# Order of three stretches of a fused attention and mixture-of-experts kernel on one Trainium2 core

## What is computed

```python
x = x + tanh(g_xattn) * attention(layernorm(x), ctx)   # x: 8 x 112 x 256, ctx: 8 x 375 x 192
x = x + tanh(g_ffn) * experts(layernorm(x))            # top-1 of 8 experts, W: 8 x 256 x 256, bias
# attention: q, k, v projections with biases, softmax(q k / 4) v for 16 heads, then Wo, bo
# experts: softmax gate, argmax, place in the expert by cumulative count, dropped beyond 112
```

## Time and profile before

| what | us |
|---|---|
| median of 3 runs | 185.61 (184.95 to 186.53) |
| the profiled execution | 185.55 |
| its span, from the first to the last instruction | 183.8 |
| PE busy | 169.8 |
| DVE busy | 128.7 |
| POOL busy | 86.4 |
| ACT busy | 80.7 |

### The profile page before, as it was taken

How to read it: one execution, slowest core, us unless ns; L and a number is a source line. 1 busy time by engine, 2 the same in 40 slices (tenths; PEclk the granted TensorE clock), 3 DMA queues, 4 the chain that set the end, 5 groups by cost and what they waited for, 6 DMA issues and landing times.

```text
span 183.8 us, 4666 instructions
## 1 busy us (share of the span) xinstructions
PE 169.8 (92%) x1799; PEld 119.6 (65%) x1799; DVE 128.7 (70%) x325; ACT 80.7 (44%) x174; POOL 86.4 (47%) x112
## 2 busy tenths in 40 slices
PE   7999979997899999999999999799689989999992
PEld 2557446674587768868766886666467876468740
DVE  5878787838278859858875988895876547755642
ACT  2114131377546817645671764356357760013100
POOL 7297948346991198563027007631040057304650
PEclk9999999999999999999999999999999999999998
DMA  5995838687375357616737532886050005387220
GB/s 153 303 259 123 187 86 208 164 197 186 92 167 136 128 129 168 211 52 156 208 100 168 162 115 69 194 255 220 0 154 4 0 23 180 117 239 199 65 61 25
DMA packets 26029, 26.04 MB, mean 142 GB/s; under 512 B 9677, under 2 KB 24409, under 8 KB 26008
## 3 DMA queue, kind: packets, MB, share of 16 engines
q1 hardware_dynamic: 24322, 23.04, 48.0%
q0 software_dynamic: 864, 2.07, 3.7%
q10 hardware_dynamic: 822, 0.64, 1.3%
HBM read 8.89 MB, written 5.06 MB: 76 GB/s over the span
## 4 chain that ended last, share of the span: by engine, by line
PE 65%; DVE 13%; SPq 5%; DMA 5%; issue 4%; ACT 4%; POOL 3%; DVEq 0%; ACTq 0%; POOLq 0%
PE pj L500 9%; PE pv L576 8%; PE sT L561 7%; PE pj L517 6%; PE sc L531 6%; PE sT L832 4%; PE sc L832 3%; PE pj L813 3%; DVE nmax L1097 3%; DMA ctx_sb<-in_ctxT 3%; PE pj L509 3%; PE misc L590 3%; SPq L364 2%; DMA x_sb<-in_x 2%; SPq L358 2%
## 5 line engine op out<-in xcount | busy, mean ns | idle before, releaser
L1097 DVE TENSOR_REDUCE nmax<-sc 112x1 f32<-112x375 f32 x112 | 58.4, 539 | 23.6 <-PE sc L531 19.6
L945 ACT ACTIVATE prob<-sT 128x448 f32<-128x448 f32 (+1 forms) x96 | 50.0, 545 | 38.1 <-PE sT L561 37.5
L561 PE MATMUL sT<-q,k 128*128 128x112 bf16 x384 | 31.7, 213 | 2.6 <-ACT prob L945 2.0
L1412 POOL TENSOR_SCALAR ve<-mv 112x1 f32<-112x1 f32 (+2 forms) x12 | 2.9, 238 | 66.2 <-DVE mv L1167 58.9
L531 PE MATMUL sc<-k,q 126*128 126x375 bf16 x104 | 31.7, 325 | 1.5 <-DVE nmax L1097 1.3
L561 PEld LDWEIGHTS sT<-q,k 128*128 128x128 bf16 x384 | 24.3, 98 | 13.2 <-ACT prob L945 4.8
L500 PE MATMUL pj<-ctx_sb,wk_sb 128*128 128x375 f32 x64 | 23.3, 485 | 0.9 <-DVE rest_q L1085 0.6
L576 PE MATMUL pv<-prob,v_sb 128*32 128x112 f32 (+1 forms) x768 | 21.8, 261 | 0.0
L576 PEld LDWEIGHTS pv<-prob,v_sb 128*32 128x32 f32 (+1 forms) x768 | 18.0, 110 | 3.6 <-issue 2.7
L517 PE MATMUL pj<-wv_sb,ctx_sb 128*128 128x256 f32 (+1 forms) x72 | 18.9, 384 | 0.0
L1428 POOL TENSOR_TENSOR parts_k<-rest_k,parts_k 128x750 bf16<-128x750 f32 x8 | 12.5, 1562 | 7.1 <-ACT parts_k L899 7.1
(11 more groups left out here) (178 smaller groups left out, 276.6 us busy)
## 6 DMA issues: line engine op xcount, KB each, us to landing
k<-parts_k SPq DMA_DIRECT2D x48, 187.5 KB, 3.0
...
```

The source lines that it names most:

```text
L561: mm = pe.matmul(st[n % 2][:, j * NQ:(j + 1) * NQ], k6_flat[:, b % RING, from_key:from_key + CK], q6[:, b % RING, h, :], start=True, stop= ...
L945: nc.scalar.activation(prob[0:rows_here, n, :], st[n % 2][0:rows_here, 0:4 * NQ], ACT.Exp, scale=SCALE).then_inc(s_p, 1)
L1097: nc.vector.tensor_reduce(nmax[:, h:h + 1], scores_bank(b, i)[0:NQ, 0:NK], axis=AX.X, op=ALU.max, negate=True).then_inc(s_max, 1)
```

## The change

- Start: ACT's queue sends the first keys' weights ahead of x0, PE makes both halves of the first keys ahead of the transposes of x0, and ACT copies both ahead of the transposes. DVE makes the first set of queries before it normalises batches 1 and 2 and the other three after. Batch 0's K and Q move ahead of its V on PE and ACT, and K ahead of the third and fourth first scores. POOL sets the ones in `v_sb` earlier, and the warming products before the keys read `prob` instead of `v_sb`.
- Turns: the scores of heads 0 to 3 of the next batch stand in the last slots of each turn (slots 9 to 11 in turn 1, 10 and 11 in the others), the rest of a batch's heads from slot 0 on. The maxima are split in slot 8 and turned in slot 9.
- After the turns: batch 6 starts with head 4; the turn of its maxima and batch 7's first scores move ahead, and units 8 to 11 of batch 5 stand in one row.
- End: the last pair of experts of batch 7, one product pair into one bank before, becomes two products in two banks.

```diff
 
 EARLY = 10
 REST_HEADS = ((10,), (11,), (12,), (13,), (14,), (15,), (), (), (), (), (), ())
-HEADS = ((0, 1), (2, 3), (4, 5), (6, 7), (), (8, 9), (10,), (11, 12), (), (13, 14, 15), (), ())
+HEADS = ((4, 5), (6, 7), (8,), (9,), (), (10, 11), (12,), (13, 14), (15,), (), (), ())
+NEXT_HEADS = (((),) * 9 + ((0,), (1,), (2, 3)), ((),) * 10 + ((0, 1), (2, 3)))
 
...
 
 K_AT, Q_AT, V_AT = (0, 1), (2, 3), (7, 9, 10)
-PV_AT, WO_AT, X2T_AT, LOGITS_AT, MAX_AT = (0, 6), 5, 1, 3, (8, 11)
+PV_AT, WO_AT, X2T_AT, LOGITS_AT, MAX_AT = (0, 6), 5, 1, 3, (8, 9)
 HI_AT, MID_AT, VE_AT, X2E_AT = (2, 3), (6, 7), (9, 9), 1
 
-REST_AT, TURN_AT, SUMS_AT, SCALE_AT, BACK_AT, ADD_AT, STAT_AT, SPLIT_AT = (5, 5), 1, 1, 2, 3, 7, (9, 11), (6, 9)
...
 
 UNIT = tuple((n,) for n in range(UNITS))
 LAST, LATE = B - 1, B - 2
...
@@ -72,7 +73,8 @@
 
 
 def heads_in(t, n):
-    return (REST_HEADS if t == 1 else HEADS)[n]
+    own = (REST_HEADS if t == 1 else HEADS)[n]
+    return [(t, h) for h in own] + [(t + 1, h) for h in at(NEXT_HEADS, t)[n]]
 
 
 def at(table, t):
...
         turned_last_max = (misc[0:H, 256:256 + NQ], sc[1][0:H, 0:NQ])
-        dense_banks = ((sc[0], sc[1], st[0], st[1]), (st[0], st[1], pv, sc[0]))
+        dense_banks = ((sc[0], sc[1], st[0], st[1]), (st[0], st[1], pv))
+
+        def dense_at(tile, e):
+            if tile == 1 and e >= 6:
+                return sc[e - 6][0:NQ, 0:D]
+            return dense_banks[tile][e // 2][0:NQ, e % 2 * D:(e % 2 + 1) * D]
 
         block = stack.enter_context(nc.Block())
 
...
             pe.wait_ge(s_dconst, 1)
             pe.wait_ge(s_ctx[0], 16)
             first_keys(0)
+            first_keys(1)
             pe.wait_ge(s_ident, 1)
             turn_xn(0)
-            first_keys(1)
             pe.wait_ge(s_wqh, 16)
             pe.wait_ge(s_xnTe, 1)
             first_queries()
@@ -643,15 +650,15 @@
             pe.wait_ge(s_qz, 4)
             project_q(1, 0)
             project_q(1, 1)
+            project_k(0, 0)
+            first_scores(2)
+            project_k(0, 1)
+            first_scores(3)
+            project_q(0, 0)
+            project_q(0, 1)
             pe.wait_ge(s_wv, 16)
             project_v(0, 0)
             project_v(0, 1)
-            first_scores(2)
-            project_k(0, 0)
-            first_scores(3)
-            project_k(0, 1)
-            project_q(0, 0)
-            project_q(0, 1)
             pe.wait_ge(s_rest, queries_of(1))
             project_v(0, 2)
             pe.wait_ge(s_ve, 2)
...
@@ -735,36 +742,33 @@
                 for u in units:
                     scores_T(b, u)
 
-            late_scores(6, 0, 1)
+            late_scores(6, 4, 5)
             half_of_probs_v(4, 1)
-            late_scores(6, 2, 3)
+            late_scores(6, 6, 7)
             pe.wait_ge(s_rest, 2 * B)
             pe.wait_ge(s_ve, 2 * LATE)
             project_v(6, 0)
-            late_scores(6, 4, 5)
+            late_scores(6, 8, 9)
             pe.wait_ge(s_mrows, LATE)
             turn_xn2(3)
             late_units(5, 0, 1)
-            late_scores(6, 6, 7)
+            late_scores(6, 10, 11)
             project_v(6, 1)
             logits(3)
-            late_scores(6, 8, 9)
+            late_scores(6, 12, 13)
             through_wo(4)
             late_units(5, 2)
-            late_scores(6, 10, 11)
+            late_scores(6, 14, 15)
             project_v(6, 2)
             late_units(5, 3)
-            late_scores(6, 12, 13)
+            turn_max(6)
             late_units(5, 4, 5)
-            late_scores(6, 14, 15)
+            late_scores(7, 0, 1)
             half_of_probs_v(5, 0)
+            late_scores(7, 2, 3)
             late_units(5, 6, 7)
-            turn_max(6)
-
-            late_scores(7, 0, 1)
-            late_units(5, 8, 9)
-            late_scores(7, 2, 3)
-            late_units(5, 10, 11)
+
+            late_units(5, 8, 9, 10, 11)
             half_of_probs_v(5, 1)
             late_scores(7, 4, 5)
             late_units(6, 0)
...
@@ -825,8 +829,6 @@
                         pe.wait_ge(s_read, 2 * n + 6)
                     if n == 2:
                         pe.wait_ge(s_x1, B)
-                    if n == 3:
-                        pe.wait_ge(s_xinTe, E)
                 bank = dense_banks[tile][n]
                 for c in range(2):
                     pe.matmul(bank[0:NQ, :], x2T[:, B - 2 + tile, c, :],
@@ -836,6 +838,14 @@
                     mm = pe.matmul(bank[0:NQ, e * D:(e + 1) * D], pick[:, 2 * n + e, :], be_rows[:, :],
                                    start=False, stop=True, skip_group_check=True)
                 mm.then_inc(s_dense, 1)
+
+            def last_dense(e):
+                if e == 6:
+                    pe.wait_ge(s_xinTe, E)
+                at = dense_at(1, e)
+                for c in range(2):
+                    pe.matmul(at, x2T[:, LAST, c, :], wT_sb[:, e, c, :], start=(c == 0), stop=False)
+                pe.matmul(at, pick[:, e, :], be_rows[:, :], start=False, stop=True).then_inc(s_dense, 1)
 
             turn_last_max(1)
             late_units(7, 0)
@@ -885,12 +895,13 @@
             product(7)
             dense(1, 1)
             dense(1, 2)
-            dense(1, 3)
+            last_dense(6)
+            last_dense(7)
 
...
             leave_first_keys(0)
+            leave_first_keys(1)
             leave_xnT(0)
-            leave_first_keys(1)
             leave_xnT(1)
             leave_hi_k(1)
             leave_hi_q(1)
             leave_mid_k(1)
             leave_mid_q(1)
-            leave_v01(0)
             leave_hi_k(0)
             leave_hi_q(0)
+            leave_v01(0)
             leave_v2(0)
             leave_mid_k(0)
             leave_mid_q(0)
...
             nc.vector.memset(q6_flat[:, 1, :].bitcast(F32), 0.0).then_inc(s_qpad, 1)
+            nc.vector.memset(q6_flat[:, 0, :].bitcast(F32), 0.0).then_inc(s_qpad, 1)
             dve.wait_ge(s_row, 1)
             link(nc.vector.tensor_scalar(side_i[:, :], row_no[:, :], 4, 1, ALU.logical_shift_right,
                                          ALU.bitwise_and))
@@ -1232,17 +1244,17 @@
             link(nc.vector.tensor_scalar(side[:, 0:1], side[:, 1:2], -1.0, 1.0, ALU.mult, ALU.add))
             dve.wait_ge(s_x, 16)
             statistics(0, 1)
-            nc.vector.memset(q6_flat[:, 0, :].bitcast(F32), 0.0).then_inc(s_qpad, 1)
+            nc.vector.memset(q6_flat[:, 2, :].bitcast(F32), 0.0).then_inc(s_qpad, 1)
             normalise(0, 0, 1)
             dve.wait_ge(s_ident, 1)
             nc.vector.tensor_copy(ident_b[:, :], ident[0:NQ, 0:NQ]).then_inc(s_dconst, 1)
-            nc.vector.memset(q6_flat[:, 2, :].bitcast(F32), 0.0).then_inc(s_qpad, 1)
             dve.wait_ge(s_x12, 16)
             statistics(1, 3)
-            normalise(1, 1, 3)
             dve.wait_ge(s_qf, 1)
             dve.wait_ge(s_bqc, 16)
-            for n in range(4):
+            first_queries_of(0)
+            normalise(1, 1, 3)
+            for n in range(1, 4):
                 first_queries_of(n)
             for i in range(6):
...
 
-            late_max(6, 0, 1)
+            late_max(6, 4, 5)
             turn_heads(4)
-            late_max(6, 2)
+            late_max(6, 6)
             invert_sums(4)
             scale_heads(4)
-            late_max(6, 3)
+            late_max(6, 7)
             turn_back(4)
-            late_max(6, 4, 5, 6, 7, 8, 9, 10)
+            late_max(6, 8, 9, 10, 11, 12, 13)
             add_x(4)
-            late_max(6, 11)
+            late_max(6, 14)
             sums_2(4)
-            late_max(6, 12)
+            late_max(6, 15)
             variance_2(4)
-            late_max(6, 13, 14, 15)
             split_max(6)
+            leave_max_rows(6)
             late_max(7, 0)
-            leave_max_rows(6)
             late_max(7, 1, 2, 3)
...
@@ -1363,15 +1374,14 @@
 
             def combine(tile, e):
                 b = B - 2 + tile
-                bank = dense_banks[tile][e // 2]
-                dve.wait_ge(s_dense, 4 * tile + e // 2 + 1)
+                dve.wait_ge(s_dense, 4 * tile + e // 2 + 1 + (tile == 1 and e == 7))
                 if e == 0:
                     dve.wait_ge(s_mix, tile + 1)
                 else:
                     dve.wait_ge(s_read, 8 * tile + e)
                 so_far = rows[:, b, X1:X1 + D] if e == 0 else last[tile][:, :]
                 nc.vector.scalar_tensor_tensor(
-                    last[tile][:, :], bank[0:NQ, e % 2 * D:(e % 2 + 1) * D], mix[:, tile, e:e + 1],
+                    last[tile][:, :], dense_at(tile, e), mix[:, tile, e:e + 1],
...
@@ -1473,6 +1483,7 @@
             link(nc.gpsimd.memset(bq_rows[:, :].bitcast(F32), 0.0))
             nc.gpsimd.memset(ones_b[:, :].bitcast(F32), TWO_ONES).then_inc(s_ones, 1)
             nc.gpsimd.memset(k6_flat[:, 1, :].bitcast(F32), TWO_ONES).then_inc(s_kpad, 1)
+            nc.gpsimd.memset(v_sb[:, :, :, :, HD:32], 1.0).then_inc(s_vones, 1)
             first_rstd(0, 0, 1)
```

(1 more changed line is left out.)

21 lines of the change are left out of this document (11 added, 10 removed).

## The result

| | before | changed |
|---|---|---|
| median, first measurement (4 runs each), us | 185.56 | 191.12 (190.55 to 192.64) |
| ratio, 95% interval | | 1.0308 (1.0228 to 1.0387) |
| median, second measurement (13 and 6 runs) | 185.86 | 189.96 (189.44 to 192.08) |
| ratio, 95% interval | | 1.0261 (1.0213 to 1.0309) |

The change makes the kernel slower by 2.6 to 3.1%; 188.6 us had been forecast, with a range to 190.2.

The account below looks back on a forecast made before the run. PE itself was taken to bound turns 2 to 5. The terms 2.1 + 0.5 - 0.3 + 0.3 + 0.9 - 0.5 = +3.0 on 185.55 us gave 188.6 us, range 185.6 to 190.2.

Parts of the forecast that it names:

- The price of the bank: Scores in batches 1 to 6: a PSUM bank comes back about 0.95 us after its score was issued.
- Turn ends, the largest term: Ends of turns 2 to 5: scores wait 0.43 and 0.09 us for banks, 0.52 per turn, +2.1 us together.
- turn 1: Its four extra scores fall into gaps at no cost; the bank wait at its end costs +0.5 us (0 to 0.8).
- One wait that goes: Turn 5: the K product's 0.3 us wait for its context disappears, -0.3 us.
- The stretch after the turns: From 111.32 us: fewer scores of batch 6 against new waits, +0.3 us, bounds -1.8 and +1.0.
- The chain of 115.76: Late stretch: PE's 1.12 us wait on PV, turn, invert, scale and maximum stays the same, only starting later.
- Head 5's wait: Second score of the late stretch finds its bank read late, costing 0.3 us.
- The start: From first keys to K of batch 2: reordered keys, x0 transposes, queries and V cost +0.9 us, bounds -0.3 and +1.4.
- V behind the queries: Start: V's first two chunks, now after batch 0's queries, hold PE 1.75 us before K of batch 2.
- x0's landing: Start: x0 arriving later, behind the keys' weights, is covered by PE's key work; uncovered, up to a microsecond.
- The clock: Granted clock at 1.2 GHz over one turn would double its 15.63 us, the whole some 204 us; chance 0.02.
- The end: Last product pair split into two banks, so one DVE addition runs beside the second product: -0.5 us (0 to -0.6).

Follow-up runs that it names:

- after_apart: The changed kernel with the last of the four next heads moved from the end of turns 1 to 4 into the next turn's first slot; 189.16 us, ratio 1.0186.
- after_pool: The changed kernel with GpSimd's rest of batch 7's keys and queries queued ahead of normalising batch 3; 190.00 us, ratio 1.0264.
- after_late: The changed kernel with batch 6's score 9 behind the transposes and two units, and its turn of the maxima behind PV; 189.71 us, ratio 1.0194.
- the halves: Runs of the kernel before with parts of the new start; the one moving only batch 0's V behind its K and Q: 185.85 us, ratio 1.0030.
- start_keys: The kernel before with the new start except V's move, so V stays ahead of batch 0's K and Q; 187.41 us, ratio 1.0065.
- start_x0: The kernel before with the new start except V's move, and x0 still loaded ahead of the keys' weights; 187.12 us, ratio 1.0100.
- turns_alone: The kernel before with only the four next-batch heads at turn ends and the late stretch's lists; start and end as before; 189.44 us, ratio 1.0198.
- after_long: The changed kernel with only two next-batch heads at the end of turns 1 to 4, one each side of V; 188.08 us, ratio 1.0112.
- best2: The kernel before with new end, POOL's early rest of batch 7, two early heads a turn around V, late lists two scores shorter; 184.63 us, ratio 0.9976.

## Why the prediction was right in its direction and too small

- **The price of the bank** holds: 0.44 and 0.10 in turn 3 against 0.43 and 0.09, the same at the other turn ends, and 0.96 between two scores of one bank in after_apart. "Turn ends, the largest term" measures 2.2 where 2.1 was forecast, and turn 1 0.5 where 0.5 was. Two things were wrong beside it. "One wait that goes" is 0.50, not 0.3: the row's 0.3 leaves out that the score ahead of it occupies PE for half of its duration only. And turn 3's cast beside POOL, 0.39, stands in no term. The two have opposite signs, so that the sum (2.1 + 0.5 - 0.3 = 2.3 against 2.6) is off by less than the cast alone: that is luck.
- **"The stretch after the turns"** is the first step that failed: +0.3 against +0.9. Its sentence "The chain of 115.76 (PV, turn, invert, scale, maximum) is the same and only starts that much later" was wrong. Starting elsewhere, the scaling fell deeper into POOL's 1.60 us operation: 1.20 instead of 0.81, so 1.51 instead of 1.12, +0.39 that the sum does not have. after_pool takes the collision away and wins 0.8. Head 5's wait came (0.36 against 0.3), and so did the one in front of the turn of the maxima (0.65 in the row and 0.17 of modelled end, 0.8 against 0.9). What is left of the 0.92 for the saved scores is 0.7. In the second profile two pairs of batch 5's units wait 0.44 (130.17) and 0.20 for ACT, in front of which the kernel before does not wait. That this makes the missing 0.2 is likely by after_late, where 0.5 of the 1.2 came through, but it is not shown by itself.
- **"The start"** is the second: +0.9 against +1.2. The first queries lose 0.86 against the first keys, not 0.73; batch 0's queries gain 1.20 on them, not 1.53 (14.20 before, 13.00 after). "V behind the queries" loses 1.54 (3.85 to 5.39), not 1.75. The term was built as keys +0.7, V's gap -1.5, V +1.75; the halves show that V's two terms nearly cancel (+0.26 alone, nothing beside the keys), and that the keys' half by itself has the whole 1.2 (start_keys), most of it, 0.86, by the order of keys and transposes (start_x0). The parts are off by +0.13, +0.33 and -0.21, so here too some of the error cancels. That x0's landing is covered was right to within 0.2 (start_x0).
- **The clock** had 0.02 and cost the first profile 1.66. It is not part of the change: the same wait of 1.51 left the clock at its upper level in the second profile and in three versions. The Trainium skill, TensorE: Matmul & The Clock Gate, section "A second HAM failure mode: psum-queue depth-cycling", has short pauses while cycling banks as a cause of such swings. By that rule the versions with more bank waits should fall more often. Here the old turns, with no such waits at their ends, fall in 33 of 136 executions, the four kernels with all of these waits (the changed kernel, turns_alone, after_late, after_pool) in 3 of 28, and the three with fewer (after_apart, after_long, best2) in none of 24, so these runs do not bear the rule out. What decides when it falls stays open.
- **The end** came as forecast (-0.59 between its own rows).

Without the falls the five other runs of the second measurement have their median at 189.9: 1.3 above the forecast, made of 0.6 in the late stretch, 0.3 in the start, 0.3 in the turns and scatter. The median of the first measurement, 191.12, stands higher by the falls in two of its four executions and, in its other two, by 0.7 of which no run shows the origin.
